# Moving two rows of maxima into the stacked queries from ACT's queue instead of SP's, in a decoder layer on one Trainium2 core

## The reference, cut to what matters

```python
q = (query @ Wq).reshape(b, sq, 32, 32)      # 32 heads of 32
k = (key @ Wk).reshape(b, sk, 8, 32)         # 8 key/value heads, each used by 4 heads
v = (value @ Wv).reshape(b, sk, 8, 32)
scores = jnp.einsum('bhqd,bhkd->bhqk', q, k) * 32 ** -0.5
probs = jax.nn.softmax(scores, axis=-1)
out = jnp.einsum('bhqk,bhkd->bhqd', probs, v)
out @ Wo
```

## Time and profile before

| what | value |
|---|---|
| runs of the kernel | 2575.43, 2580.15, 2583.21 us; median 2580.15 us |
| the profiled execution's own time | 2575.51 us |
| its span, first to last instruction | 2573.6 us |
| mean granted clock of TensorE | 0.975 |
| busy over the span | PE 95%, DVE 49%, ACT 41%, POOL 54% |
| `attend_pass`, first to last score matmul | 1851 to 2322 us |

### The profile page before, as it was taken

One profiled execution on the slowest core, in us unless ns is written; L12 is line 12 of the kernel. 1 busy time (PEld: TensorE's weight loads), 2 busy tenths in 40 slices (PEclk: granted clock), 3 DMA queues, 4 the chain that ended last, 5 costly groups with the idle time before them and its releaser, 6 DMA issues. The chain is left out here.

```text
span 2573.6 us, 33218 instructions
## 1 busy us (share of the span) xinstructions
PE 2432.6 (95%) x12861; PEld 2123.8 (83%) x12874; DVE 1268.9 (49%) x1779; ACT 1043.6 (41%) x1531; POOL 1402.1 (54%) x626
## 2 busy tenths in 40 slices
PE   9999999999999999999999999999987777788998
PEld 9999999988999889998899988999865555555775
DVE  4762205860029720178300693445476666664665
ACT  2112235432346333373333633233376666672211
POOL 5334245855448664467554684454387776672221
PEclk9999999999999999999999999999998888898999
DMA  6565522333322343233432233799765555546773
GB/s 209 169 183 182 194 104 101 110 113 126 113 99 102 117 132 113 99 107 121 125 116 102 99 107 111 216 290 294 193 169 159 163 148 134 135 119 160 178 175 91
DMA packets 254446, 371.75 MB, mean 144 GB/s; under 512 B 126640, under 2 KB 178864, under 8 KB 254032
## 3 DMA queue, kind: packets, MB, share of 16 engines
q1 hardware_dynamic: 254288, 369.61, 47.5%
HBM read 290.15 MB, written 78.70 MB: 143 GB/s over the span
## 5 line engine op out<-in xcount | busy, mean ns | idle before, releaser
L994 POOL TENSOR_TENSOR gp_w_lo<-cy_raw,gp_w_hi 128x1024 fp32r<-128x1024 f32 (+2 forms) x299 | 721.2, 2413 | 606.4 <-ACT gp_w_hi L869 605.8
L185 PE MATMUL gp_acc<-gp_x_hi,gp_w_hi 128*128 128x448 f32 x1504 | 558.1, 371 | 2.6 <-ACT gp_row L920 2.5
L187 PE MATMUL gp_acc<-gp_x_hi,gp_w_lo 128*128 128x448 f32 x1504 | 549.7, 365 | 0.0
L186 PE MATMUL gp_acc<-gp_x_lo,gp_w_hi 128*128 128x448 f32 x1504 | 549.6, 365 | 0.0
L869 ACT CAST gp_w_hi<-cy_raw 128x1024 fp32r<-128x1024 f32 (+2 forms) x300 | 307.1, 1026 | 311.7 <-PE gp_acc L187 305.4
L1457 POOL TENSOR_TENSOR ap_e_lo<-ap_e,ap_e_hi 125x1344 fp32r<-125x1344 f32 x109 | 331.2, 3066 | 134.5 <-DVE ap_e_hi L1538 103.0
L185 PEld LDWEIGHTS gp_acc<-gp_x_hi,gp_w_hi 128*128 128x128 f32 x1504 | 282.8, 188 | 25.8 <-ACT gp_row L920 4.0
L187 PEld LDWEIGHTS gp_acc<-gp_x_hi,gp_w_lo 128*128 128x128 f32 x1504 | 282.5, 188 | 22.0
L186 PEld LDWEIGHTS gp_acc<-gp_x_lo,gp_w_hi 128*128 128x128 f32 x1504 | 282.9, 188 | 20.7
L1524 DVE TENSOR_REDUCE cy_n_max<-ap_p_s 112x2 f32<-112x750 f32 x240 | 221.1, 936 | 120.4 <-PE ap_p_s L1595 117.6
L483 DVE TENSOR_REDUCE gp_sel_unit<-gp_keys 112x4 f32<-112x2048 f32 x4 | 9.1, 2286 | 547.1 <-ACT gp_keys L881 547.1
(11 more groups left out here) (207 smaller groups left out, 4411.9 us busy)
## 6 DMA issues: line engine op xcount, KB each, us to landing
cy_raw<-in_w_gu SPq DMA_DIRECT2D x172, 512.0 KB, 3.2
cy_raw<-in_w_d SPq DMA_DIRECT2D x80, 512.0 KB, 3.5
cp_c_raw<-in_ctx_t SPq DMA_DIRECT2D x32, 750.0 KB, 6.6
cy_raw<-in_w_q SPq DMA_DIRECT2D x32, 512.0 KB, 4.6
q_scratch<-gp_q_out SPq DMA_DIRECT2D x64, 224.0 KB, 6.2
cy_qs<-q_scratch SPq DMA_DIRECT2D x64, 224.0 KB, 3.4
k_scratch<-cp_k_out SPq DMA_DIRECT2D x32, 376.0 KB
cy_ks<-k_scratch SPq DMA_DIRECT2D x64, 188.0 KB, 4.2
```

The costliest lines, as they stand in the source:

```text
L185: nc.tensor.matmul(out, wh, xh, start=first, stop=False)
L186: nc.tensor.matmul(out, wh, xl, start=False, stop=False)
L187: return nc.tensor.matmul(out, wl, xh, start=False, stop=last)
L994: last = nc.gpsimd.tensor_tensor(o, i, hi.bitcast(F32), ALU.subtract)
```

## The change

The two DMAs of `put_max` are issued one at a time, by whichever engine calls it. In `attend_pass` the call leaves SP's queue (the turn h = 6), and ACT issues them instead: the row of `nm_hi` behind the exponential of step 20 and the row of `nm_lo` behind the exponential of step 21, each with a wait for the semaphore of its source. For batch 0 they stay in SP's queue, with a wait of its own for the first of them.

```diff
-    def put_max(self, sp, n):
-        p, stack = n % 2, 3 * HD
-        sp.wait_ge(self.nml, n + 1)
-        for row, src in ((stack, self.nm_hi), (stack + 1, self.nm_lo)):
-            sp.dma_start(self.qs[p][row:row + 1].bitcast(F32).rearrange("o f j m q -> o (f j m) q"),
-                         src[:].bitcast(F32)).then_inc(self.nm_put, 16)
+    def put_max(self, eng, n, i):
+
+        eng.dma_start(self.qs[n % 2][3 * HD + i:3 * HD + i + 1].bitcast(F32).rearrange("o f j m q -> o (f j m) q"),
+                      (self.nm_hi, self.nm_lo)[i][:].bitcast(F32)).then_inc(self.nm_put, 16)
...
                 if p == 32:
-                    cy.put_max(sp, 0)
+                    sp.wait_ge(cy.nmh, 1)
+                    cy.put_max(sp, 0, 0)
+                    sp.wait_ge(cy.nml, 1)
+                    cy.put_max(sp, 0, 1)
...
-                    if h == TURN_AT // KT and n + 1 < B:
-                        cy.put_max(sp, n + 1)
...
                     if x == TURN_AT + 1 and n + 1 < B:
                         max_hi(n + 1)
+                    if x == TURN_AT + 2 and n + 1 < B:
+                        act.wait_ge(nmh, n + 2)
+                        cy.put_max(act, n + 1, 0)
+                    if x == TURN_AT + 3 and n + 1 < B:
+                        act.wait_ge(nml, n + 2)
+                        cy.put_max(act, n + 1, 1)
```

## The result

The changed kernel takes 2561.09 us (median of 6 runs, 2551.74 to 2564.40) against 2578.94 us of the kernel before (6 runs, 2575.43 to 2583.21); the ratio is 0.9924, 95% interval 0.9902 to 0.9946. It is faster by 18 us (0.8%, clear of the scatter of the runs), where some 90 were forecast, and the time lies outside the range given. The profiled execution has a span of 2562.5 us, 11 less than before; its attention, from the first score matmul to batch 15, takes 436.8 us (1854.02 to 2290.82) against 451.0 before, so 14 us come from there. The passes before it, which the change does not touch, took 2.8 us longer in this execution (the first score matmul comes at 1854.02, not 1851.25).

What follows compares the result with a forecast made beforehand. PE's wait for the nm_lo row at each attention batch start was taken as the bound. Savings of 1.8, 39.8 (batches 1 to 7), 6.9 (8), 36.1 (9 to 13) and 2.7 us (14) made 87: 2490 us, range 2468 to 2535.

Steps and rivals of the forecast that it cites:

- What bounds the kernel: Attention, step 0 of each batch: PE waits for the nm_lo DMA, 88.4 us in 15 waits; no engine is the bound.
- the landing from ACT's queue: nm_lo row, issue to arrival: taken as 3.0 us, bounds 2.1 and 7.5, cutting PE's wait from 6.5 to 1.2 us.
- rival B: Row's landing: another queue does not pass transfers ahead; landing near 7.3 us, 4 us won, about 2572; chance 0.12.
- The issue time of the row: nm_lo row in ACT's order: issued 0.6 us earlier than from SP.
- ACT's two issues: ACT, ahead of steps 21 to 23: 0.6 us each, costed at 0, or 0.3 us a batch for n < 8.
- Rival C: ACT held 2.3 us by each issue, exponentials late, batches 3.9 us longer, about 2630 us; chance 0.05.
- The clock: PE steps 0 to 2 behind the long wait: slow clock costs 1.5 us a batch, gone with a 1.2 us wait.
- What is late next: Batches once the wait shrinks: 24.7 us each for n < 8, set by POOL, and 23.7 later.
- Rival A: Landing half cured (about 5 us) or ACT tight: waits of 3.2 us remain, 67 us saved, 2510; chance 0.14.

## Why the prediction was wrong

*What bounds the kernel:* right. It was the landing of the row, and the five engines full of values behind it; the control with 115 partitions and the run with 112 show it. Without both obstacles the wait is gone.

*The step that failed:* the landing from ACT's queue. I took 3.0 us between bounds of 2.1 and 7.5, on the reasoning that a row in a queue of its own waits only for pieces of 6.2 KB under way, 0.26 us each, "a few such turns". It measured 7.1, and the wait fell from 6.5 to 5.0 us a batch, not to 1.2. In the changed kernel all 125 pieces of the values had started before the row's last ten, and ended 4.3 to 5.1 us after its issue. With the values issued only 0.5 us ahead of it, the row waited for some 12 pieces on each of the five engines, and not for one or a few. The trace had already said that the engines and not SP's queue were full, and I had it in rival B with a chance of 0.12. The assumption about the length of a turn had no row behind it, and the whole forecast of 87 us hung on it. 3.0 us is the landing one gets from ACT once the values are spread and the fetches held: 3.2 in that run, whose 2487.69 us is the forecast's 2490. What the sum made of a 3 us landing was right; the change alone did not give that landing.

The Trainium skill ("DMA: Bandwidth & Descriptors", Queues, rings and completion order) lets engines switch between rings after a whole packet, of about 9 to 17 descriptors and at most 64; I had read a turn as one piece, and "nearer 3 than 7.5" does not follow from the page. At 0.26 us a piece, 9 to 17 pieces are 2.3 to 4.4 us, so with the 2.0 of an undisturbed landing an estimate by that page is 4.3 to 6.4 us. The trace agrees: some 12 pieces went first, and 5.4 us were measured ahead of batch 15, where nothing is fetched beside the values. Its section Issuing engines are not separate DMA queues says that another issuing engine saves the issue time alone. The trace of the changed kernel agrees nearly: the landing went from 7.5 to 7.1 us, and the rest of the gain was earlier issue.

*The issue time of the row:* mis-sized the other way. I took 0.6 us earlier; it is 1.03, because ACT issues at the start of the exponential and not behind it. That is why rival B, right in its mechanism, was too slow with 2572: its 7 x 0.6 = 4 us should have been 14 x 1.03 = 14, which gives 2562. That this is the measured time is in part luck: the landing gave 0.4 us a batch more, and the longer slow stretch took 6 us back. B also had nothing won for n < 8, behind the rounding of weights; the row's lead over PE is 2.27 to 2.30 us there as later.

*ACT's two issues:* right at 0. They take 0.51 us in the median (`nm_hi` up to 0.61) under a running exponential of 0.54. Rival C (2.3 us an issue) did not occur; the longest of the 15 issues of `nm_lo` was 0.514 us.

*The clock:* the link was right, the size too small. With the wait the slow steps stayed, as they had to; the filled wait shows them worth 27 us, some 2 a batch where I had 1.5.

*What is late next:* 24.7 us a batch for n < 8 was exact once the wait was gone (172.8 us for batches 1 to 7 in the run with rows from ACT, fetches held and values spread, against the 172.9 of my sum). Batches 9 to 13, taken at 23.7, were 24.0 in that run and 23.1 in the one with rows from SP; batch 8, with POOL's backlog, was 25.3 and 25.8 against 24.7.

*Rival A* (a landing half cured, 2510) has the time of the run with spread values and rows from SP (2510.09 us), not that of the change; its waits of 3.2 us and landing of 5 were 2.4 and 3.3 there, so the same number is chance.

Open is what sets the length of a turn, and whether it is counted in pieces or in bytes. The two runs with values behind the rows and the two orders within SP's queue say that the time of issue decides in the main. The 1.1 us between the landings 3.2 (rows from ACT) and 2.1 (from SP, nothing ahead) goes with the packets of that run: ahead of the row's last piece all 64 pieces of the fetch issued 0.5 us before it had started, and 18 to 42 of the 64 of the next one, issued 0.03 us behind it.

## What to carry to other kernels

A small transfer on the critical path that takes long to land is cured by changing what is issued ahead of it; the queue that issues it did little here (7.1 us against 7.5). So compare its landing with that of the same transfer when nothing else runs (here 2.1 us against 7.5), and look for a large transfer whose partitions leave most DMA engines idle. Cut such a transfer so that all engines carry it (112 + 13 partitions for 125: 61 us here with the rows from ACT, 65 from SP), and issue the small one ahead of the bulk (a further 25 us from SP's queue). A matmul engine that waits some 5 us pays again behind the wait, here some 2 us each time.

## What the runs showed of the hardware

- A transfer of 125 or 115 partitions loads five of the 16 DMA engines (share 0.32 at 120 GB/s and 0.28 at 114), and a 14 KB row issued behind it landed in 7 us in place of 2; with 112 + 13 partitions the same bytes ran at a share of 0.97 and 361 GB/s, and the row landed in 3.3 to 4.0.
- A row issued from ACT 0.5 us behind the values of SP's queue waited for some 12 of their 25 pieces on each of the five engines (2.9 us at 0.24 each) and passed the others.
- A DMA issued from ACT takes 0.51 us in the median (0.65 for `nm_lo` in the run with issue one step later), under a running activation whose length stays 0.54 to 0.55 us.
- Granted clock behind waits of PE of 4.5 to 7 us: 0.50 and 0.59 over the next 4 to 5 us, the lower of its two levels for most of them. Behind a wait of 3.01 us steps 0 to 2 ran at 1.00 in 2.61 us; behind one of 2.13 us (batch 5, rows from ACT, values spread) they took 3.87 us at 0.65, and behind one of 1.80 us (batch 10, fetches held too) 4.17 us at 0.59. So waits of 1.8 to 3 us went both ways, and what decides is open. With 20 idle matmuls in the wait the clock stayed at 1.00.
